# Two cross-attention layers with expert layers on one Trainium2 core: maxima through a masked 64-row product, normalisations on ScalarE, row sums on GpSimd, and the context's split halves kept in DRAM

## The reference, cut to what matters

```python
x = x + _L0_xattn_ref(_layernorm(x), ctx_1024, Wq, bq, Wkv, bkv)     # 16 heads of 16
x = x + _L0_ffn_ref(_layernorm(x), ...)                              # each row to 1 of 8 experts
x = x + _L1_xattn_ref(_layernorm(x), ctx_1024, Wq, ..., g1, b1)      # 8 heads of 32
x = x + _L1_ffn_ref(_layernorm(x), ...)                              # each row to 2 of 8 experts
# inside both attentions
scores = einsum('bqhd,bkhd->bhqk', Q, K) * scale
attn = softmax(scores, axis=-1)
out = einsum('bhqk,bkhd->bqhd', attn, V)
# the second one goes on
O = layernorm(qh + out) * g0 + b0
O = layernorm(O + relu(O @ Wo.T + bo)) * g1 + b1
```

## Time and profile before

| | |
|---|---|
| median of 3 runs | 2270.12 us (2255.2 to 2271.07) |
| profiled execution | 2271.3 us, span of its instructions 2268.6 us |
| PE busy over the span | 1862.0 us (82%) |
| DVE busy | 1394.0 us (61%) |
| POOL busy | 987.0 us (44%) |
| ACT busy | 799.5 us (35%) |
| granted TensorE clock, mean | 0.906 |
| DMA | 102.05 MB, mean 45 GB/s |

### The profile page before, as it was taken

How to read it: one execution, slowest core, us unless ns; L and a number is a source line. 1 busy time by engine, 2 the same in 40 slices (tenths; PEclk the granted TensorE clock), 3 DMA queues, 4 the chain that set the end, 5 groups by cost and what they waited for, 6 DMA issues and landing times. The chain is left out here.

```text
span 2268.6 us, 44822 instructions
## 1 busy us (share of the span) xinstructions
PE 1862.0 (82%) x14222; PEld 1319.0 (58%) x14223; DVE 1394.0 (61%) x2612; ACT 799.5 (35%) x1535; POOL 987.0 (44%) x1128
## 2 busy tenths in 40 slices
PE   6988888888888749999698888888887268888884
PEld 4656565665566426666477777777775135555552
DVE  5877777777778442222277777777776624444442
ACT  3545445444454302222254444444442011111110
POOL 4444444444444201111355555555553026666663
PEclk8999989899899769999799999999997579999998
DMA  4111111100000041111202121111110232222223
GB/s 108 37 45 35 46 51 35 37 23 17 25 17 13 9 181 33 32 32 32 71 22 69 47 66 50 42 48 30 30 31 8 80 89 38 38 38 37 37 39 79
DMA packets 54161, 102.05 MB, mean 45 GB/s; under 512 B 11842, under 2 KB 37674, under 8 KB 50698
## 3 DMA queue, kind: packets, MB, share of 16 engines
q1 hardware_dynamic: 37754, 78.87, 10.9%
q0 software_dynamic: 16352, 22.47, 5.4%
HBM read 79.78 MB, written 24.93 MB: 46 GB/s over the span
## 5 line engine op out<-in xcount | busy, mean ns | idle before, releaser
L825 DVE TENSOR_REDUCE a_mx<-a_SM 100x2 f32<-100x722 f32 x384 | 348.6, 908 | 90.8 <-PE a_SM L406 74.4
L1424 PE MATMUL e_PH<-w,e_xT 128*128 x712 | 327.5, 603 | 6.0 <-DVE e_ab L1556 2.9
L666 POOL TENSOR_TENSOR a_rstd<-a_ve,a_half_neg 100x1 f32<-100x1 f32 x224 | 129.6, 579 | 393.4 <-DVE a_ve L784 393.4
L629 ACT ACTIVATE a_Pr<-a_ST 120x800 f32<-120x800 f32 (+1 forms) x288 | 241.6, 839 | 160.9 <-PE a_ST L433 160.9
L406 PE MATMUL a_SM<-a_KTb,a_QMb 64*100 64x361 bf16 x768 | 141.1, 364 | 131.3 <-DVE a_mx L825 125.8
L711 POOL TENSOR_TENSOR a_DM<-a_neg_ident,a_mx 100x800 bf16<-100x800 bf16 x96 | 147.7, 1538 | 166.3 <-DVE a_mx L825 166.3
L1424 PEld LDWEIGHTS e_PH<-w,e_xT 128*128 128x128 f32 x712 | 135.2, 194 | 142.0 <-issue 139.1
L444 PE MATMUL a_M<-a_Pr,a_V 120*32 120x100 f32 (+3 forms) x4608 | 202.4, 279 | 0.3 <-ACT a_Pr L629 0.3
L1345 POOL COPY e_gidx<-toks 128x1 int32 (+1 forms) x89 | 48.4, 544 | 300.5 <-PE e_PX L1413 205.7
L406 PEld LDWEIGHTS a_SM<-a_KTb,a_QMb 64*100 64x100 bf16 x768 | 48.2, 122 | 217.0 <-DVE a_mx L825 172.4
L444 PEld LDWEIGHTS a_M<-a_Pr,a_V 120*32 120x32 f32 (+3 forms) x4608 | 156.5, 133 | 24.0 <-issue 15.7
(11 more groups left out here) (186 smaller groups left out, 4299.5 us busy)
## 6 DMA issues: line engine op xcount, KB each, us to landing
w<-in_E_w SPq DMA_DIRECT2D x24, 1024.0 KB, 5.0
a_ct<-in_ctx SPq DMA_DIRECT2D x64, 362.0 KB, 3.1
keep_rows<-a_keep SPq DMA_DIRECT2D x64, 100.0 KB
tile_rows<-e_y SPq DMA_DIRECT2D x32, 128.0 KB
b_rows<-in_E_b SPq DMA_DIRECT2D x1, 4096.0 KB
sums<-X SPq DMA_DIRECT2D x1, 3200.0 KB
out<-sums SPq DMA_DIRECT2D x2, 1600.0 KB, 9.4
X<-in_x SPq DMA_DIRECT2D x1, 2800.0 KB
```

The source lines that it names most:

```text
L629: nc.scalar.activation(dst.rearrange("p (j q) -> p j q", j=2), ST[0:n, (b.p * NS + s) % 2, :, 0:4 * LQ], ACT.Exp, scale=SCALE).then_inc(ex ...
L666: nc.gpsimd.tensor_tensor(rstd[k][:], ve[k][:], half_neg[:], ALU.pow).then_inc(rstd_ready[k], 1)
L825: V_.tensor_reduce(pair, SM[0:LQ, :, 0:LK], AX_X, ALU.max).then_inc(max_done, 1)
L1424: last = nc.tensor.matmul(PH[:, h, :], xT[:, c, :], rhs, start=(c == 0), stop=(c == DC - 1))
```

## The change

Four things are changed in `attention`, for both layers.

1. Maxima. `diagonals` goes. DVE's `repeat_max` copies each head's maximum over the 16 or 32 columns of that head into `mxr` (two copies, bfloat16). PE's `max_columns`, the first thing of step b, transposes `mxr` by two products with `neg_ident` (now -1/HD on its diagonal) into the PSUM tile ST; ACT copies them to `mxT`; POOL's `masked_max` multiplies by the mask into `MXM`, with the layout of `QM`. The ones product in `scores` then has 64 rows of `ones_bf` and `MXM` instead of 100 rows.
2. Normalisations. `xh`, `xp` and `keep` are made by ACT as x * rstd + (-mean * rstd); POOL makes the new column `nmr`. In layer 0 the second layer norm's factor `rstd2` is made from the first one's variance by POOL, without statistics of `xp`. The copy `q_hi` moves from DVE to ACT.
3. Row sums. POOL's `value_bias`, `attended` and `attended_twice` (layer 0) and `query_bias` (layer 1) do sums that DVE did.
4. Context. Layer 0 stores `ch` and `cl` of each batch to DRAM (SP, `keep_split`); layer 1 loads them, with no `ct`, `high_context` or `low_context`.

```diff
         def _(sp):
+            def keep_split(b):
+                sp.wait_ge(cl_ready, b.count(1, 1))
+                sp.dma_start(dram("ctx_high", b), ch[b.p][:].bitcast(F32)).then_inc(split_stored[b.p], 16)
+                sp.dma_start(dram("ctx_low", b), cl[b.p][:].bitcast(F32)).then_inc(split_stored[b.p], 16)
             def load(b):
+                if layer == 1:
+                    if b.low >= 2:
+                        sp.wait_ge(v_ps, b.count(2, -2))
+                    sp.dma_start(ch[b.p][:].bitcast(F32), dram("ctx_high", b)).then_inc(split_loaded[b.p], 16)
+                    sp.dma_start(cl[b.p][:].bitcast(F32), dram("ctx_low", b)).then_inc(split_loaded[b.p], 16)
+                    return
                 if b.low >= 2:
-                    sp.wait_ge(cl_ready, b.count(1, -1))
+                    keep_split(b.plus(-2))
...
+            if layer == 0:
+                for b in (NB - 2, NB - 1):
+                    keep_split(fixed(b))
+                    sp.wait_ge(split_stored[b % 2], 32 * (NB // 2))
...
         def _(pe):
+            def max_columns(b):
+                pe.wait_ge(mxr_ready, b.count(1, 1))
+                for c in range(DC):
+                    last = nc.tensor.matmul(ST[:, 1, 0, c * LQ:(c + 1) * LQ], mxr[:, c, :], neg_ident[:],
+                                            start=True, stop=True)
+                last.then_inc(mxT_ps, 1)
             def scores(b, s):
                 if kt == 0:
-                    pe.wait_ge(dm_ready, b.count(EIGHTS, eight + 1))
+                    pe.wait_ge(mxm_ready, b.count(EIGHTS, eight + 1))
...
                 for j in range(2):
-                    h = 8 * eight + 4 * j
-                    nc.tensor.matmul(ST[0:n, buf, j, 0:4 * LQ], ones_bf[:, 0:n], DM[:, h:h + 4, :],
-                                     start=True, stop=False)
+                    rows = place(8 * eight + 4 * j)[0]
+                    nc.tensor.matmul(ST[0:n, buf, j, 0:4 * LQ], ones_bf[rows, 0:n],
+                                     MXM[rows, C * eight:C * eight + C, :, :], start=True, stop=False)
...
         def _(act):
+            def normed(out, k, b, src):
+                act.wait_ge(nmr_ready[k], b.count(1, 1))
+                return nc.scalar.activation(out, src, ACT.Identity, bias=nmr[k][:], scale=rstd[k][:, 0:1])
+            def max_columns(b):
+                act.wait_ge(mxT_ps, b.count(1, 1))
+                act.wait_ge(mxm_ready, b.count(EIGHTS))
+                nc.scalar.activation(mxT[:], ST[:, 1, 0, 0:DC * LQ].rearrange("p (c q) -> p c q", c=DC), ACT.Copy
+                                     ).then_inc(mxT_ready, 1)
...
         def _(pool):
+            def masked_max(b, e):
+                pool.wait_ge(mxT_ready, b.count(1, 1))
+                if b.low >= 1:
+                    pool.wait_ge(st_ps, b.count(NS, 3 * e + 3 - NS))
+                C = DC // EIGHTS
+                nc.gpsimd.tensor_tensor(
+                    MXM[:, C * e:C * e + C],
+                    mxT[:, C * e:C * e + C, :].unsqueeze(2).to_broadcast([128, C, HT, LQ]),
+                    mask_bf[:].unsqueeze(1).unsqueeze(3).to_broadcast([128, C, HT, LQ]), ALU.mult).then_inc(mxm_ready, 1)
             def step(b, fr, ahead, back, tail):
+                if back:
+                    for e in range(EIGHTS):
+                        masked_max(b, e)
+                if tail and layer == 0:
+                    attended(prev)
+                    power(1, prev)
                 if fr:
                     low_parts(nxt)
...
         def _(dve):
+            def repeat_max(b):
+                dve.wait_ge(max_done, b.count(NP, NP))
+                dve.wait_ge(mxT_ps, b.count(1))
+                for c in range(DC):
...
+                    last = V_.tensor_copy(out, heads.unsqueeze(len(heads.shape)).to_broadcast(list(out.shape)))
+                last.then_inc(mxr_ready, 1)
             def step1(b, fr, ahead, back, tail):
...
-                    if ahead and j == 1:
+                    if ahead and j == 0:
                         input_stats(nxt2)
-                    if ahead and j == 2:
-                        input_rows(nxt2)
...
+                if fr:
+                    repeat_max(nxt)
                 if back:
                     normalise(b)
```

More of the change, by code:

```diff
@@ L631, in step @@
                                              ).then_inc(exp_done, 1)
-                    if ahead and s == 0:
+                    if ahead and s == 0 and layer == 0:
                         high_context(b.plus(2))
+                    if tail and layer == 0 and s == 1:
+                        attended_rows(b.plus(-1))
+                    if tail and layer == 0 and s == 2:
+                        kept(b.plus(-1))
                     if tail and s == 2 + (1 - layer):
@@ L636, in step @@
                         copy_out(prev, 0, RC + DC if prev.low >= LAG else DC)
+                    if ahead and s == 4 - 2 * layer:
+                        input_rows(b.plus(2))
                 if back:
@@ L643, in step @@
                     copy_k(b.plus(2), 0)
+                if layer == 1 and tail and b.plus(-2).low >= 0:
+                    kept(b.plus(-2))
             act.wait_ge(loaded, FIRST_LOADED)
@@ L728, in step @@
                     residual1(prev2)
-                if tail and layer == 0:
-                    power(2, prev)
                 if fr and layer == 0:
                     masked_low(nxt, 0)
-                    diagonals(nxt, 0)
                 if ahead:
                     power(0, nxt2)
-                if ahead:
+                if ahead and layer == 0:
                     low_context(nxt2)
+                if tail and layer == 0:
+                    attended_twice(prev)
                 if ends:
@@ L741, in step @@
                     masked_low(nxt, EIGHTS - 1)
-                    diagonals(nxt, EIGHTS - 1)
+                if fr and layer == 0:
+                    value_bias(nxt)
+                if fr and layer == 1:
+                    query_bias(nxt)
                 if tail and layer == 1:
```

224 lines of the change are left out of this document (146 added, 78 removed).

## The result

The changed kernel takes 2250.3 us (median of 20 runs, 2227.2 to 2277.5), the kernel before in the same comparison 2268.7 us (20 runs, 2253.7 to 2276.4). The ratio is 0.9913, 95% interval 0.9888 to 0.9937: just under 1% faster, where I forecast 1% slower. The ratio leaves out runs more than 1.5% above the fastest of their kernel, of which the changed kernel had four. The profiled execution has a span of 2256.1 us, 12.5 us less than before.

The account below looks back on a forecast made before the run. TensorE was taken to bound both attentions, a tenth of each period spent waiting. From 2271.3 us, -93 (first attention), +109 (second) and +4 (DMA) gave 2291 us, no clear change on the slow side; range 2207 to 2352.

Parts of the forecast that it names:

- the clock term of the first attention: First attention: half of the 2.15 us a batch clock loss stays, 1.1 us, bounds 0 and 2.15.
- The narrower 2250 to 2330: Whole kernel: the forecast's own spread in us, said to come from both stages' bounds in opposite directions.
- 17.7 of work and 2.05 of waits: First attention, TensorE a batch at full clock: 17.7 us work plus 2.05 us waits, together 19.75 us.
- 0.18 saved per pair: Ones products before each score tile: 64-row halves overlap, 0.30 us for 0.48, six times 0.18 = 1.1 us less.
- the step's end: TensorE waits for the last maximum and its copies: 2.0 us, 0.77 filled, 1.25 us idle.
- The forecast of +109: Second attention: 23.0 us a batch, 3.5 more than 19.5; over 31 periods +109 us, bounds +56 and +142.
- The wait for the mask product: Second attention: masked_max stands behind power(2) and the gather on GpSimd, so TensorE waits 2.4 us, bounds 1.5 and 3.2.
- VectorE's relief is spent on the reordering: Second attention, first to third pair: rstd wait goes, input_stats comes in; 5.0 us as before, TensorE waits 2.1 us.
- +4 us forecast: End of the first attention: it waits for the last four context stores, +4 us, bounds 0 and 10.
- The faster one: Second attention: GpSimd's queue is free before TensorE needs the mask product; 20.3 us a batch, 2207 us total; chance 0.28.
- The clock rival: Second attention's idle time brings more 1.2 GHz, 24.1 us a batch; first may keep its loss; 2357 us; chance 0.20.
- The third, no overlap of the halves: Ones products: two 64-row products do not overlap, the pair stays at 0.48 us; 2322 us; chance 0.12.

Follow-up runs that it names:

- the 128-row run: Changed kernel with the ones product over 128 rows, ones in one half and zeros in the other, both attentions: 2280.0 us, ratio 1.005 to the kernel before.
- The runs with load: Changed kernel plus useless VectorE statistics behind the first attention's fourth and sixth maximum: six and six, 2292.3 us; then 11 and 17, 2516.3 us.
- the two pairs of runs: Context split again in the second attention, no stored halves: on the changed kernel 2221.4 us; with mask product first and input_stats late 2078.1, against 2078.3 with halves.
- the first experiment on this attention: Changed kernel with the second attention's mask product ahead of power(2) and the gather in GpSimd's queue: 2182.0 us, ratio 0.9617 to the kernel before.
- another arrangement: Changed kernel with the second attention's maxima by diagonals: 2256.7 us with early input_stats, 2123.2 us with input_stats back behind the second maximum.
- the version without low clock: Changed kernel, second attention with mask product ahead of power(2) and the gather, and input_stats back behind the second maximum: 2078.3 us, ratio 0.9168.
- four of the experiments: Changed kernel with, in the second attention: input_stats late (2167.0 us), mask product first (2182.0), gather alone moved (2208.2), or diagonals (2256.7).

## Why the prediction was wrong, by its own steps

**The step that failed is the clock term of the first attention**: "Half of the old clock loss stays by my guess, 1.1 us". Nothing of it stays: the granted clock is 1.00, outside the 0.88 to 0.97 that I had named as a sign of being wrong. The period came out 1.5 us under the forecast (19.34 for 20.9), 1.1 of it by this term. Over 31 periods the term is 34 us. The bound that I named for it (no loss, -127) is what happened, and with it in its place the sum would have been about 2257 us. That this meets the measured time, and that the first attention is 125.7 - 93 = 33 us better than forecast, is in part luck. The period was 0.4 us better for other reasons, which would be some 14 us more, but the short batches at the ends took that back; and the second attention came out 8 us worse, the rest 8 us better. The range of 2207 to 2352 held the time. The narrower 2250 to 2330 does not follow from the bounds: those of both stages in opposite directions give 2271 and 2290, and in the same direction 2204 and 2357.

**Work and waits of the first attention.** I had 17.7 of work and 2.05 of waits; measured are 17.07 and 2.27. The ones product was mis-sized (0.18 saved per pair, measured 0.30 of busy time), and the loops gave part back as waits, as the 128-row run shows. The waits themselves are in their places: 0.29 at short loops against 0.1 forecast, 0.84 at the step's end against 1.25.

A batch before without low clock shows an error inside the split of the old period:

```profile
272.30:294.91 22.61, 19.07 (x212) 13.21 (x211) 18.45 (x29) 11.35 (x20) 10.60 (x11) 1.00 0.20 67
294.91:319.51 24.60, 21.72 (x213) 15.23 (x212) 18.64 (x29) 11.35 (x20) 10.74 (x11) 0.86 0.07 19
```

22.6 us at full clock, not the 21.75 that I got by taking half of the slow time off. Low clock for 28% of 24.6 us is 6.9 us and lengthens TensorE's work by 2.65 us, but the batch by 2.0: waits took up the rest. So the old loss was 23.9 - 22.6 = 1.3 us a batch, and the change brought 22.6 to 19.3, 3.3 us at full clock, where I had reckoned 2.0. The second attention has the same error, smaller: its full-clock batches before take 18.5 to 18.6 us, not the 18.1 that I had, so its old loss was about 1.0 us and not 1.4. In the waits of the first attention I had also left out those for `affs`, 26.1 us in all.

**Why VectorE's relief counted.** The loops of score rows shrank from 2.75 and 4.12 to 1.33 and 2.13 us. The runs with load show that enough work on VectorE between the maxima brings the low clock back, and the first of them that the total of idle time does not decide. Which of the moved operations counted is not shown: xh did not, and the sums and the copy q_hi were not put back one by one.

**Second attention.** The forecast of +109 stands on terms that mostly held. At full clock I had 21.3 us, measured are 21.2. The wait for the mask product is 2.0 (2.4 forecast), the step's end 1.04 (1.25), first to third pair 5.05 (5.0), the wait in it 2.7 (2.1). The clock costs 23.74 - 21.2 = 2.5 us against my 1.7, inside its bound of 2.8. Over the whole stage that gives +117 for +109; by the periods alone it would be +131. "VectorE's relief is spent on the reordering" is right and was too mild: the late place of `input_stats` is worth 3.3 us a batch. I priced it as keeping the old distance and did not see that it was the most costly line of those tried: undoing it gives 83 us, moving the mask product 68.

**DMA.** +4 us forecast, about 3.5 in the two pairs of runs. The part between the attentions is still 3.9 us shorter than before, for other reasons, which I have not sought.

**The rivals.** The faster one (GpSimd's queue free early) did not happen: the wait is there in the trace. What it describes was made by hand in the first experiment on this attention and gave 2182 us, better than its 2207, though only by the first attention: the second took 21.13 us a batch, where the rival had 20.3. The clock rival held for half of its claim: in the second attention the low time rose from 14 to 24%, in the first it vanished. And it does not fall in every batch: 5 of the 22 have none. The third, no overlap of the halves, is excluded by the rows: the pair takes 0.34 us and not 0.55, and the next product starts 0.02 us behind it and not 0.48.

The Trainium skill, page "TensorE: Matmul & The Clock Gate", section "HAM oscillation — how this bites in real kernels", counts the price of the throttled time as its half. In the second attention the trace agrees: 7% of clock missing in a batch of 23.00 us is 14% of low time, 3.2 us, half of which is 1.6, and the batch is 1.8 us longer. In the first attention before it is less, as worked out above, where waits stand beside the slow work.

## What to carry to other kernels

Before a wait is priced at its own length, look at what the granted clock does behind it: here 1.5 us of statistics in one loop cost 3.3 us a batch, and 4.7 in another arrangement. Split a period into single batches with and without low clock, rather than into mean clock times mean period. And when an operation goes to an in-order queue, put it where its own input comes ready; here GpSimd stood idle for 2.30 us ahead of the power, where the 0.86 us of the mask product had room, and the product stood behind the power and the gather, 2.9 us later.

## What of the hardware was not expected

- A clock loss of 18% of the time went to zero with only 1.3 us less idle time in a batch (3.5 to 2.3), while 3.6 us of idle time, differently spread, left it at 1%. In these kernels it matters where the idle time lies, and not only how much there is.
- The same second attention gave 24%, 19%, 19% and 23% of low time in the profiles of four kernels that differ only in the first (the changed one, xh on VectorE, both loads). The changed kernel's 20 runs spread over 2.2%, the version without low clock over 0.3% in 4 runs. Low clock alone does not make a kernel noisy: with 9, 22, 30 and 42% of it in the second attention, four of the experiments spread over only 0.15 to 0.32% in their 4 to 10 runs. In the profile of the changed kernel the low time differs from batch to batch, from 0 to 46%; with 42% it is the same in all but the first of the batches 5 to 26.
- 64-row products overlap their neighbours: a pair of ones products and the next score product start 0.02 us apart behind a score row, where the 128-row form has 0.48 us between them.
- The gather takes GpSimd's queue for 1.09 us of issue and 0.92 us of standing idle before it, behind a copy of 0.18 us.
